# Experts over token lists in DRAM instead of all tokens through all experts

## The chip, the cores and the metric

One core of a Trainium2 chip runs the kernel. The metric is device time in microseconds (us). The engines are TensorE (PE; PEld is its loading of weights), VectorE (DVE), ScalarE (ACT), GpSimd (POOL) and SyncE (SP), which issues most DMAs. Each engine works through its own list of instructions in order; semaphores tie the lists together.

## The reference

2048 tokens of 256 features pass a cross-attention layer with 16 heads over 1601 keys (causal mask and key mask, sigmoid gate, residual), and then a mixture of 8 experts of which each token takes two:

```python
x = x + xattn(layernorm(x), ctx, ctx, mask, Wq, Wk, Wv, Wo, Wg, bg)
xf = layernorm(x)
scores = softmax(xf @ gate_w)                      # (T, 8)
top_scores, top_idx = top_k(scores, 2)
scale = zeros((T, 8)).at[arange(T)[:, None], top_idx].set(top_scores)
xs = scale.T[:, :, None] * xf[None]                # zero rows where not chosen
h = silu(einsum('etd,edh->eth', xs, w1)) * einsum('etd,edh->eth', xs, w3)
x = x + einsum('eth,ehd->etd', h, w2).sum(axis=0)  # hidden size 128
```

An expert gives exactly zero for a token that did not choose it, as silu(0) * 0 = 0.

## The kernel before

The tokens are cut into four chunks of 512 (`CH`), taken in the order 1, 2, 3, 0 (`ORDER`); the chunk 0 is last and has the fewest visible keys. Attention runs over 16 groups (a chunk and four heads): maxima of the scores ("mx", PE and DVE L1303), then per tile of 128 keys the scores ("st", PE L1578), their exponentials (ACT L1160) and the product with the values ("pv", PE L1600). POOL turns a group's maxima into rows for the scores (L1042 to L1055).

After a chunk's attention comes its router: "gT", "wo" (output projection and residual), "bn", "stat" and "norm" (layernorm; POOL's rstd L994), "xT1", "logits", and on DVE the ranks of the 8 probabilities; a rank below 1.5 keeps its probability in `scale_sb` (L1370). "sT" transposes it; it goes to DRAM and comes back as 8 rows broadcast over all partitions ("sload", SP L933).

The feed-forward is dense: for every chunk and every expert, products "a" and "b" (PE L1664 to L1666) of w1 and w3 with all 512 tokens of the chunk, scaled by the token's row on DVE (L1380, L1387), then tanh on ACT, the product of both and "y" with w2 (L1685 to L1693), which sums the 8 experts of a chunk in two banks of PSUM; "yT" transposes back and adds to `x_sb`. Full precision is kept by splitting each operand into a high and a low part (`w_hi`, `w_lo`, `x_hi`, `x_lo`, `h_hi`, `h_lo`), so each product is three matmuls; 32 steps (chunk, expert) of 18 matmuls of 512 columns.

`make_plan` orders all steps ahead of time: a list of streams, each with its needs (`needs`), planned durations (`pe_time`, `ALONE`, `THEN`) and a patience (`PATIENCE`, "feed": 4000 ns). The next step is the one that can start first; among equals, the one whose deadline is nearest. The plan's order is the order of every engine's list; POOL's and SP's lists are sorted by planned start. The experts' weights take the place of keys in SBUF that attention has done with (`freed_by`, "ws" on POOL), and the first of the feed-forward's steps wait until all maxima are done.

Of the kernel before, what the change touches and what calls it, by code (L numbers as in the profile page):

```python
# [34 lines left out]
I32 = mybir.dt.int32  # L35
ALU = mybir.AluOpType
# [31 lines left out]
PATIENCE = {"turn": 1000, "route": 3000, "project": 6000, "weights": 0, "feed": 4000}  # L68
# [3 lines left out]
Y_BANKS = (5, 6)  # L72
# [49 lines left out]
def freed_by(ex):  # L122

    end = 4 * (KD * CH + (ex + 1) * 3 * D if ex is not None else 2 * KD * CH + E * 3 * D)
    return KEYS_LAST + (end - 1) // (4 * (KP - CH)) // 2
# [45 lines left out]
def router(c):  # L171

    return [("gT", c, 0), ("gT", c, 1), ("wo", c, 0), ("wo", c, 1), ("bn", 1, c), ("stat", 1, c),
            ("norm", 1, c), ("xT1", c, 0), ("xT1", c, 1), ("logits", c), ("rexp", c), ("rank0", c), ("rank1", c),
            ("rank", c), ("sT", c)]


def feed_forward():

    steps, todo = [], [(c, e) for c in ORDER for e in range(E)]  # L180
    for i, (c, e) in enumerate(todo):
        if i:
            steps.append(("hl", *todo[i - 1]))
        steps.extend([("a", c, e), ("b", c, e), ("h", c, e)])
        if e == 4 and POS[c] + 1 < NC:
            steps.append(("xs", ORDER[POS[c] + 1]))
        if i >= 3 and todo[i - 3][1] == E - 1:
            steps.extend(finish(todo[i - 3][0]))
        if i >= 2:
            steps.append(("y", *todo[i - 2]))  # L190
            if todo[i - 2][1] == E - 1:
                steps.append(("ycopy", todo[i - 2][0]))
    steps.extend([("y", *todo[-2]), ("hl", *todo[-1]), ("y", *todo[-1]), ("ycopy", ORDER[-1]), *finish(ORDER[-1])])
    return steps


def finish(c):

    return [(kind, c, part) for part in range(2) for kind in ("yT", "out")]


def consumer(e):
# [6 lines left out]
    if kind in ("v", "xT0", "st", "mT", "sT"):  # L209
        return "act"  # L210
    if kind in ("gT", "xT1"):
        return "act" if POS[e[1]] < NC - 1 else "dve"
    return "dve" if kind in ("gate", "mx", "oT", "wo", "logits", "a", "b", "yT") else None


def pe_time(e):
# [7 lines left out]
    if kind == "pv":  # L224
        q0, q1 = shares(e[2], e[3])[e[4]]
        return 4 * PASS * (q1 - q0) + 60
    return {"sel": 230, "v": 860, "gate": 1720, "wo": 1720, "xT0": 450, "xT1": 450, "gT": 450, "oT": 450, "sT": 450, "mT": 230,
            "logits": 900, "a": 1380, "b": 1380, "y": 1400, "yT": 500}.get(kind, 0)


def read_time(e):
# [8 lines left out]
    if kind in ("v", "logits"):  # L240
# [1497 lines left out]
```

## Time and profile before

| | |
|---|---|
| time, three runs | 677.1, 680.0, 682.3 us (median 680.0) |
| span of the profiled execution | 676.9 us; its own time is not listed apart from the three |
| PE | 644.6 us busy (95%), 5320 matmuls |
| PEld | 393.0 us (58%) |
| DVE | 471.3 us (70%) |
| ACT | 379.5 us (56%) |
| POOL | 230.4 us (34%) |
| mean granted PE clock | 0.981 of 2.4 GHz |

The span runs from the first to the last instruction. Busy times of PE are modelled: matmuls overlap, and the sum of single durations is more than the time that they take. The page's slices show DVE full until about 425 us and at 10 to 80% afterwards; PE is full from 40 us to the end.

### The profile page before, as it was taken

The page shows a single profiled execution, that of the slowest core. Times are in us where ns is not written, and L with a number is a line of the kernel's source. Part 1 is how long each engine was busy: PE and PEld are TensorE (multiplying, and loading weights), DVE is VectorE, ACT ScalarE, POOL GpSimd, SP SyncE. Part 2 cuts the span into 40 slices and gives each one's busy share as a digit, 9 for nine tenths or more (in the row PEclk, how much of TensorE's full clock was granted, in tenths as well). Part 3 has the DMA queues.
Part 4 walks back from the last instruction along what each step waited for, and adds up shares of the span by engine and source line. Part 5 has one row for each costly group of instructions (what it writes and reads, how often), then busy time and mean ns, then how long its engine had stood idle before and what let it go on. Part 6 is the DMA issues. An engine that isn't in the chain of part 4 may idle for free.

```text
span 676.9 us, 13559 instructions
## 1 busy us (share of the span) xinstructions
PE 644.6 (95%) x5320; PEld 393.0 (58%) x5320; DVE 471.3 (70%) x981; ACT 379.5 (56%) x778; POOL 230.4 (34%) x283
## 2 busy tenths in 40 slices
PE   7887999999999999999999999999999999979997
PEld 3363565555565545554565556455456766768885
DVE  6637779998989999999989987412205533676454
ACT  2221456766646676667646677877784565123332
POOL 5005212522123115021005033385434434536662
PEclk9878799999999999999999899999999999999999
DMA  6985982010260000010093010102101021104100
GB/s 170 234 133 115 138 144 31 2 22 24 69 68 1 3 1 3 1 65 2 14 161 109 2 34 3 35 2 78 32 32 32 17 63 49 31 16 109 48 32 31
DMA packets 29305, 36.58 MB, mean 54 GB/s; under 512 B 5833, under 2 KB 16457, under 8 KB 29242
## 3 DMA queue, kind: packets, MB, share of 16 engines
q1 hardware_dynamic: 26248, 34.53, 24.6%
q8 instruction: 42, 0.69, 0.4%
q10 hardware_dynamic: 946, 0.92, 0.4%
q0 software_dynamic: 2048, 0.27, 0.3%
q14 instruction: 21, 0.17, 0.1%
HBM read 25.58 MB, written 8.06 MB: 50 GB/s over the span
## 4 chain that ended last, share of the span: by engine, by line
PE 45%; DVE 12%; ACT 3%; POOL 2%; issue 1%; DVEq 0%; ACTq 0%; POOLq 0%
PE bank L1600 9%; DVE pmax L1303 9%; PE bank L1578 8%; PE bank L1664 4%; PE bank L1666 4%; PE bank L1665 4%; PE bank L1429 3%; PE bank L1545 3%; PE bank L1685 2%; PE bank L1686 2%; ACT probs L1160 2%; PE bank L1688 2%; DVE xn_sb L1274 1%; PE bank L1610 1%; PE bank L1583 1%
## 5 line engine op out<-in xcount | busy, mean ns | idle before, releaser
L1160 ACT ACTIVATE probs<-bank 128x512 f32<-128x512 f32 (+4 forms) x592 | 283.2, 555 | 147.0 <-PE bank L1578 87.5
L1303 DVE TENSOR_REDUCE pmax<-bank 128x1 f32<-128x512 f32 (+6 forms) x640 | 322.7, 574 | 29.4 <-PE bank L1549 15.9
L1578 PE MATMUL bank<-qaug,kaug 64*128 64x512 f32 (+4 forms) x592 | 151.6, 455 | 2.5 <-DVE pmax L1303 1.1
L1600 PE MATMUL bank<-probs,vaug 128*32 128x256 f32 (+4 forms) x2048 | 142.3, 390 | 2.2 <-ACT probs L1160 1.8
L1545 PE MATMUL bank<-kaug,qaug 62*128 62x512 f32 (+6 forms) x640 | 135.0, 404 | 9.8 <-DVE stage L807 3.4
L1578 PEld LDWEIGHTS bank<-qaug,kaug 64*128 64x128 f32 (+1 forms) x592 | 66.2, 183 | 85.7 <-ACT probs L1160 29.8
L1545 PEld LDWEIGHTS bank<-kaug,qaug 62*128 62x128 f32 x640 | 76.5, 189 | 40.7 <-DVE pmax L1303 21.0
L1600 PEld LDWEIGHTS bank<-probs,vaug 128*32 128x32 f32 (+1 forms) x2048 | 52.3, 109 | 53.3 <-ACT probs L1160 18.4
L1032 POOL TENSOR_TENSOR h_lo<-v_sb,h_hi 128x512 fp32r<-128x512 f32 x31 | 40.1, 1295 | 66.3 <-ACT h_hi L1216 66.3
L1396 DVE SCALAR_TENSOR_TENSOR v_sb<-t_sb,v_sb 128x512 f32<-128x512 f32 x32 | 24.2, 757 | 45.2 <-POOL v_sb L1028 38.2
L1216 ACT ACTIVATE h_hi<-v_sb 128x512 fp32r<-128x512 f32 x32 | 20.4, 637 | 57.4 <-DVE v_sb L1396 55.5
L1042 POOL TENSOR_SCALAR nmax<-rmax 128x16 f32<-128x16 f32 x16 | 4.4, 278 | 136.3 <-DVE rmax L1311 136.1
L1665 PE MATMUL bank<-x_lo,w_hi 128*128 128x512 f32 x128 | 50.5, 394 | 0.0
L1055 POOL DMA_DIRECT2D qaug<-low_rows x64 | 34.6, 547 | 26.2 <-ACT low_rows L1167 26.2
L994 POOL TENSOR_TENSOR rstd<-var_e,minus_half 128x4 f32<-128x4 f32 x8 | 9.1, 1135 | 83.3 <-DVE var_e L1266 83.3
L1549 PE MATMUL bank<-tri_b,eye_b 64*128 64x128 bf16 (+1 forms) x416 | 37.0, 224 | 0.0
L1387 DVE SCALAR_TENSOR_TENSOR v_sb<-bank,qaug 128x512 f32<-128x512 f32 x32 | 22.1, 689 | 15.2 <-PE bank L1666 15.1
L1093 ACT ACTIVATE stage<-bank 128x512 fp32r<-128x512 f32 (+1 forms) x16 | 8.8, 551 | 37.0 <-PE bank L1429 27.1
L1583 PE MATMUL bank<-eye_b,tri_b 64*128 64x64 bf16 (+1 forms) x416 | 27.9, 195 | 0.0
L1380 DVE TENSOR_TENSOR u_even<-bank,qaug 128x512 f32<-128x512 f32 x16 | 11.0, 688 | 24.0 <-PE bank L1666 24.0
L1380 DVE TENSOR_TENSOR u_odd<-bank,qaug 128x512 f32<-128x512 f32 x16 | 11.0, 687 | 23.9 <-PE bank L1666 23.8
L1685 PE MATMUL bank<-h_hi,w_hi 128*128 128x512 f32 x64 | 26.7, 417 | 0.4 <-ACT h_hi L1216 0.4
(143 smaller groups left out, 824.4 us busy)
## 6 DMA issues: line engine op xcount, KB each, us to landing
qaug<-s_dram SPq DMA_DIRECT2D x32, 256.0 KB, 3.4
qaug<-q_parts SPq DMA_DIRECT2D x18, 256.0 KB, 9.2
q_parts<-stage SPq DMA_DIRECT2D x7, 512.0 KB, 2.9
k_parts<-stage SPq DMA_DIRECT2D x4, 512.0 KB, 5.0
w_sb<-in_w SPq DMA_DIRECT2D x4, 512.0 KB, 10.0
out<-x_sb SPq DMA_DIRECT2D x8, 256.0 KB, 2.3
ctx_sb<-in_ctx_t SPq DMA_DIRECT2D x3, 512.0 KB, 6.4
x_sb<-in_x SPq DMA_DIRECT2D x3, 512.0 KB, 6.3
```

The source lines that it names most:

```text
L1032: pool.tensor_tensor(h_lo[:, i % 2, :], v_sb[:, i % 2, :], h_hi[:, i % 2, :].bitcast(F32), ALU.subtract).then_inc(h_lo_ready, 1)
L1055: pool.dma_start(qaug[row:row + 1, p % 2, GP * g:GP * (g + 1), :].bitcast(F32), m_row[at:at + GP, :].bitcast(F32)).then_inc(m_landed[n % 4 ...
L1160: act.activation(probs[0:rows, u % NSLOT, h, off:CH], bank_of(e)[0:rows, off:CH], ACT.Exp, scale=DK ** -0.5).then_inc(act_read, 1)
L1303: dve.tensor_reduce(pmax[:, n % 2, qt, h, slot:slot + 1], bank[:, 0:w], AX_X, ALU.max).then_inc(dve_read, 1)
L1545: last.append(pe.matmul(pair[side][0][:, 0:w], qaug[b:b + ROW_MAX, p % 2, hp, P * qt:P * (qt + 1)], keys_at(b, ROW_MAX, hp, k0, w), start= ...
L1549: last = [pe.matmul(bank[:, d:w], eye_b[b:b + HALF, a + 1 - side, :], tri_b[b:b + HALF, a + 1 - side, 0:w - d], start=False, stop=(a == 1) ...
L1578: last.append(pe.matmul(pair[side][0][0:r, off:CH], keys_at(b, ROWS, hp, P * j, r), qaug[b:b + ROWS, p % 2, hp, off:CH], start=True, stop= ...
L1583: last = [pe.matmul(bank[0:r, q0:q0 + HALF], tri_b[b:b + HALF, a + 1 - side, 0:r], eye_b[b:b + HALF, a + 1 - side, HALF * a:HALF * (a + 1) ...
L1600: last = pe.matmul(psum[O_BANK][32 * h:32 * h + 32, q0:q1], vaug[0:r, col:col + 32], probs[0:r, u % NSLOT, h, q0:q1], start=(j == 0), stop ...
L1664: pe.matmul(bank[:, :], hi, x_high, start=(a == 0), stop=False)
L1665: pe.matmul(bank[:, :], hi, x_low, start=False, stop=False)
L1685: pe.matmul(dst, hi, h_hi[:, i % 2, :], start=(ex == 0), stop=False)
```

## The change

A token's normalized row is multiplied by each of its two probabilities and written to DRAM, behind the other tokens of that expert. The tokens form three sets: chunks 1 and 2, chunk 3, chunk 0 (`SETS`). For each chunk "cnt" counts on PE, with matrices of ones and of zeros and ones, how many earlier tokens of the set chose each expert; DVE makes a slot number of it for both choices of each token. "wide" makes the weighted rows (on POOL for chunks 1 and 2, on DVE for 3 and 0), and "scat" scatters them with eight indirect DMAs from POOL. "tail" (SP) writes 128 zero rows behind each expert's list, and "table" (DVE) lists for each block of 128 rows which expert it belongs to and where it starts, and for each token where its two results will be.

A set has a fixed number of blocks, two rows per token and up to one started block per expert: 23, 15 and 15, 53 in all. For a block SP reads the row's place into a register and loads 128 rows ("bl"); PE transposes them ("bx") and multiplies them, now as the stationary operand, with 256 columns of w1 and w3 of the block's expert, whose place PE reads from a register ("bab"); "bh" transposes the hidden rows, "by" multiplies with w2; SP stores the result ("bst"). The steps of a block are issued with lags 0 to 3 (`LAGS`). After a set is stored, POOL gathers both results of each token ("back", four indirect DMAs for 256 tokens), and DVE adds them to `x_sb` ("add", "out").

The dense steps ("sT", "sload", "xs", "a", "b", "h", "hl", "y", "ycopy", "yT") are gone. `row_in` and the weights lie in the keys' place. The core of the diff:

```diff
-PATIENCE = {..., "weights": 0, "feed": 4000}
+PATIENCE = {..., "weights": 0, "blocks": 4000}
+SETS = ((1, 2), (3,), (0,))
+LAGS = {"bx": 0, "bab": 1, "bh": 2, "by": 3}
+RING = 3
+COUNT = tuple(2 * TPC * len(chunks) + E - 1 for chunks in SETS)
+BLOCKS = [(s, b) for s, count in enumerate(COUNT) for b in range(count)]
+XIN, YOUT, GOT = 4, 3, 3
+W_STEP = 3 * D
+def block_steps():
+    steps, count = [], len(BLOCKS)
+    for i in range(count + max(LAGS.values())):
+        for kind, lag in LAGS.items():
+            if 0 <= i - lag < count:
+                steps.append((kind, i - lag))
+    return steps
...
-            "logits": 900, "a": 1380, "b": 1380, "y": 1400, "yT": 500}.get(kind, 0)
+            "logits": 900, "cnt": 500, "bx": 280, "bab": 760, "bh": 150, "by": 400}.get(kind, 0)
...
+THEN = {..., "scat": 8800, "back": 4400, "wide": 9800}
...
         if kind == "ws":
-            return [("xs", ORDER[0])] + all_st(freed_by(e[1])) + ...
+            return [("prologue_end",), ("mred", NC * G - 1)] + all_st(freed_by(e[1]))
+        if kind == "bl":
+            s = BLOCKS[e[1]][0]
+            return ([("table", s), ("tail", s)] + [("scat", c) for c in SETS[s]] + all_st(G * (NC - 1) - 1)
+                    + ([("bx", e[1] - XIN)] if e[1] >= XIN else []))
+        if kind == "bx":
+            return [("bl", e[1])] + ([("bab", e[1] - 2)] if e[1] >= 2 else [])
+        if kind == "bab":
+            return [("bx", e[1]), ("ws", E - 1)]
...
# SyncE
+                elif kind == "bl":
+                    i = e[1]
+                    s, b = BLOCKS[i]
+                    if b == 0:
+                        sp.wait_ge(table_ready, s + 1)
+                        sp.wait_ge(tail_out[s], 16 * (E + 1))
+                        for c in SETS[s]:
+                            sp.wait_ge(scattered[c], 16 * 2 * TPC)
+                    if i == 0:
+                        sp.wait_ge(*made(last_st[last_unit[G * (NC - 1) - 1]]))
+                    if i >= XIN:
+                        sp.wait_ge(*taken(("bx", i - XIN)))
+                    at = sp.value_load(read_i[0:1, s, b:b + 1], min_val=0, max_val=E * ROOM[s])
+                    sp.dma_start(row_in[:, i % XIN, :], sent[s][bass.ds(at, 1), :, :].rearrange("r p d -> (r p) d")).then_inc(row_landed[i % XIN], 16)
+                elif kind == "bst":
...
+                    sp.dma_start(fed[s][b, :, :], y_sb[:, i % YOUT, :]).then_inc(y_stored[i % YOUT], 16)
...
# GpSimd
+                elif kind == "scat":
...
+                    for t in range(TPC):
+                        for k in range(2):
+                            pool.wait_ge(rows_wide, 2 * TPC * POS[c] + 2 * t + k + 1)
+                            pool.indirect_dma_start(to, bass.IndirectOffsetOnAxis(ap=slots[:, c, k, t:t + 1], axis=0), wide(k, t), None
+                                                    ).then_inc(scattered[c], 16)
+                elif kind == "back":
...
+                    for r in range(YOUT):
+                        pool.wait_ge(y_stored[r], 16 * sum(1 for i in range(LAST_BLOCK[s] + 1) if i % YOUT == r))
...
+                            pool.indirect_dma_start(got[:, g % GOT, k, t, :], None, rows,
+                                                    bass.IndirectOffsetOnAxis(ap=back_at[:, k, 2 * g + t:2 * g + t + 1], axis=0)
+                                                    ).then_inc(got_landed[g % GOT], 16)
...
# ScalarE: one copy or pass per step of a block
+                    act.activation(row_hi[:, i % 2, :], bank_of(e)[:, 0:D], ACT.Copy).then_inc(row_hi_ready, 1)
...
+                    act.activation(t_sb[:, i % RING, :], bank_of(e)[:, 0:HID], ACT.Tanh, scale=0.5).then_inc(tanh_done, 1)
...
+                    act.activation(h_hi[:, i % RING, :], bank_of(e)[:, 0:P], ACT.Copy).then_inc(h_hi_ready, 1)
...
+                    act.activation(y_sb[:, i % YOUT, :], bank_of(e)[:, 0:D], ACT.Copy).then_inc(act_read, 1)
...
# VectorE, one block
+                    dve.tensor_tensor(row_lo[:, i % 2, :], bank[:, 0:D], row_hi[:, i % 2, :].bitcast(F32), ALU.subtract).then_inc(dve_read, 1)
...
+                    step(dve.scalar_tensor_tensor(out=at_sb[:, i % RING, :], in0=t_sb[:, i % RING, :], scalar=1.0, in1=bank[:, 0:HID],
+                                                  op0=ALU.add, op1=ALU.mult))
+                    dve.scalar_tensor_tensor(out=h_sb[:, i % RING, :], in0=at_sb[:, i % RING, :], scalar=0.5, in1=bank[:, HID:2 * HID],
                                              op0=ALU.mult, op1=ALU.mult).then_inc(dve_read, 1)
...
# TensorE
+                elif kind == "bx":
+                    i = e[1]
+                    pe.wait_ge(row_landed[i % XIN], 16 * (i // XIN + 1))
+                    bank = make(e)
                     for a in range(KD):
+                        last = pe.transpose(bank[:, P * a:P * (a + 1)], row_in[:, i % XIN, P * a:P * (a + 1)], ident[:, :])
                     last.then_inc(dve_full, 1)
+                    s, b = BLOCKS[i]
+                    if b == 0:
+                        pe.wait_ge(table_ready, s + 1)
+                    whose[i] = pe.value_load(whose_i[0:1, s, b:b + 1], min_val=0, max_val=E - 1)
+                elif kind == "bab":
...
                     for a in range(KD):
+                        high, low = (row[:, i % 2, P * a:P * (a + 1)] for row in (row_hi, row_lo))
+                        hi, lo = (w[:, bass.ds(whose[i] * W_STEP + D * a, D)] for w in w_all)
+                        pe.matmul(bank[:, 0:D], high, hi, start=(a == 0), stop=False)
+                        pe.matmul(bank[:, 0:D], low, hi, start=False, stop=False)
+                        last = pe.matmul(bank[:, 0:D], high, lo, start=False, stop=(a == KD - 1))
                     last.then_inc(dve_full, 1)
...
+                elif kind == "by":
...
+                    hi, lo = (w[:, bass.ds(whose[i] * W_STEP + KD * D, D)] for w in w_all)
+                    pe.matmul(bank[:, 0:D], h_hi[:, i % RING, :], hi, start=True, stop=False)
+                    pe.matmul(bank[:, 0:D], h_lo[:, i % RING, :], hi, start=False, stop=False)
+                    pe.matmul(bank[:, 0:D], h_hi[:, i % RING, :], lo, start=False, stop=True).then_inc(act_full, 1)
```

## Rows read from the trace of the kernel before

**Rows 1.** Stretches: us, busy of PE, PEld, DVE, ACT, POOL, clock, DMA, GB/s

```profile
100.00:420.00 320.00, 314.12 (x3128) 177.54 (x3124) 295.14 (x640) 213.98 (x447) 77.72 (x121) 0.99 0.18 33
436.00:607.00 171.00, 163.83 (x1288) 105.86 (x1283) 64.15 (x130) 100.31 (x215) 85.19 (x68) 1.00 0.12 35
607.00:677.00 70.00, 65.01 (x292) 52.18 (x292) 36.49 (x55) 21.14 (x35) 36.96 (x28) 0.99 0.18 53
```

**Rows 2.** One line's instructions: duration ns min/median/max, first and last start

```profile
L1303 DVE TENSOR_REDUCE pmax<-bank x640: 277/546/693, 26.7 to 433.1; 128x1 f32<-128x512 f32 x64, 128x1 f32<-128x364 f32 x48, 128x1 f32<-128x384 f32 x16, 128x1 f32<-128x128 f32 x8
```

**Rows 3.** Stretches, instructions that read or write w_hi (PE, PEld, POOL)

```profile
436.00:607.00 171.00, 69.95 (x208) 38.10 (x208) 21.06 (x16) 1.00 0.12 35
607.00:677.00 70.00, 55.76 (x176) 33.03 (x176) 0.00 (x0) 0.99 0.18 53
```

**Rows 4.** Stretches, instructions that read or write w_lo (PE, PEld, POOL)

```profile
436.00:607.00 171.00, 40.95 (x104) 19.56 (x104) 14.67 (x8) 1.00 0.12 35
607.00:677.00 70.00, 34.81 (x88) 16.53 (x88) 0.00 (x0) 0.99 0.18 53
```

**Rows 5.** Stretches with and without gaps on PE

```profile
20.00:80.00 60.00, 50.98 (x226) 30.95 (x226) 37.83 (x79) 13.88 (x28) 11.46 (x15) 0.83 0.83 160
620.00:640.00 20.00, 20.00 (x88) 16.22 (x87) 10.37 (x13) 5.93 (x10) 14.07 (x11) 1.00 0.15 54
```

**Rows 6.** Two lines' instructions: last step of the choice of experts; a normalization

```profile
L1370 DVE SCALAR_TENSOR_TENSOR scale_sb<-r_rank,r_prob x4: 191/192/193, 227.5 to 607.2; 128x32 f32<-128x32 f32 x4
...
L1274 DVE TENSOR_SCALAR xn_sb<-x_sb,stat,rstd x12: 396/410/1420, 9.1 to 594.0; 128x256 f32<-128x256 f32 x12
```

**Rows 7.** Timeline: start us, us, engine, line, operation, count

```profile
580.36 1.89 PE L1429 MATMUL bank<-wo_sb,att_t 128*128 128x256 f32 x8
...
594.43 0.85 PEld L1504 LDWEIGHTS bank<-ident,xn_sb 128*128 128x128 f32 x8 [2.54 <-DVE xn_sb L1274]
...
597.90 1.98 PEld L1429 LDWEIGHTS bank<-gw_sb,gate_sb 128*128 128x128 f32 x16
```

**Rows 8.** Instruction groups by form: count, busy us, mean ns of one, idle before

```profile
L1160 ACT ACTIVATE probs<-bank 128x128 f32<-128x128 f32 x48 | 10.5, 276 | 10.8 <-PE bank L1583 10.7
...
L1108 ACT ACTIVATE vaug<-bank 128x256 f32<-128x256 f32 x12 | 4.6, 385 | 17.8 <-PE bank L1429 17.8
...
L1323 DVE TENSOR_TENSOR att_sb<-bank,rinv 128x256 f32<-128x256 f32 x16 | 6.8, 425 | 0.6
...
L1303 DVE TENSOR_REDUCE pmax<-bank 128x1 f32<-128x128 f32 x32 | 7.3, 281 | 1.3 <-PE bank L1549 1.3
...
L1004 POOL TENSOR_SCALAR xn_sb<-x_sb,stat,rstd 128x256 f32<-128x256 f32 x20 | 24.3, 1225 | 0.4
...
L1055 POOL DMA_DIRECT2D qaug<-low_rows x64 | 34.6, 547 | 26.2 <-ACT low_rows L1167 26.2
...
L1093 ACT ACT_TABLE_LOAD x1 | 1.3, 1283 | 3.2 <-issue 3.2
```

**Rows 9.** Two lines of DMA issues on SP: duration ns min/median/max

```profile
L933 SPq DMA_DIRECT2D qaug<-s_dram x32: 319/320/441, 388.9 to 634.5; - x32
...
L939 SPq DMA_DIRECT2D out<-x_sb x8: 372/388/389, 555.5 to 674.2; - x8
```

**Rows 10.** The chain of waits around 499 us: start us, us, what

```profile
498.84 0.37 PE bank L1578 x2
...
499.27 0.29 PE bank L1578 x2
...
499.74 1.06 PE bank L1600 x16
```

**Rows 11.** DMA issues: count, KB each, median us to landing

```profile
qaug<-s_dram SPq DMA_DIRECT2D x32, 256.0 KB, 3.4
...
out<-x_sb SPq DMA_DIRECT2D x8, 256.0 KB, 2.3
...
qaug<-low_rows POOLq DMA_DIRECT2D x64, 4.0 KB, 1.6
```

More of the change, by code:

```diff
@@ L35 @@
 I32 = mybir.dt.int32
+U32 = mybir.dt.uint32
 ALU = mybir.AluOpType
@@ L67 @@
 MOST = {"st": 3, "mx": 5}
-PATIENCE = {"turn": 1000, "route": 3000, "project": 6000, "weights": 0, "feed": 4000}
+PATIENCE = {"turn": 1000, "route": 3000, "project": 6000, "weights": 0, "blocks": 4000}
 EPS = 1e-5
@@ L71 @@
 KEYS_LAST = G * (NC - 2)
-Y_BANKS = (5, 6)
+SETS = ((1, 2), (3,), (0,))
+LAGS = {"bx": 0, "bab": 1, "bh": 2, "by": 3}
+RING = 3
+SET_OF = {c: s for s, chunks in enumerate(SETS) for c in chunks}
+ROOM = tuple(TPC * len(chunks) + 1 for chunks in SETS)
+COUNT = tuple(2 * TPC * len(chunks) + E - 1 for chunks in SETS)
+BLOCKS = [(s, b) for s, count in enumerate(COUNT) for b in range(count)]
+LAST_BLOCK = tuple(sum(COUNT[:s + 1]) - 1 for s in range(len(SETS)))
+ROW = D
+XIN, YOUT, GOT = 4, 3, 3
+W_STEP = 3 * D
 Q_PARTS = (0, 0, 1)
@@ L122, in freed_by @@
 def freed_by(ex):
[L124 to L125 removed]
+    return KEYS_LAST + (4 * W_STEP * (ex + 1) - 1) // (4 * (KP - CH)) // 2
 def mate(e):
@@ L267, in make_plan @@
         "project": [[e] for p in range(NC) for e in projections(p)] + [[("prologue_end",)]],
-        "scale": [[("sload", c, ex)] for c in ORDER for ex in range(E)],
         "turn": [[("oT", n)] for n in range(NC * G)],
@@ L275, in make_plan @@
         "values": [[e] for e in values],
-        "weights": [[("xs", ORDER[0])]] + [[("ws", ex)] for ex in range(E)],
-        "feed": [[e] for e in feed_forward()],
+        "weights": [[("ws", ex)] for ex in range(E)],
+        "loads": [[("bl", i)] for i in range(len(BLOCKS))],
+        "blocks": [[e] for e in block_steps()],
+        "stores": [[("bst", i)] for i in range(len(BLOCKS))],
+        "backs": [[("back", *o)] for o in halves()],
+        "adds": [[(kind, *o)] for o in halves() for kind in ("add", "out")],
     }
@@ new lines, in _ @@
+                        dve.wait_ge(*made(("cnt", ORDER[POS[c] - 1])))
+                    dve.tensor_scalar(chosen[:, :, :], r_rank[:, POS[c], :, :], 1.5, None, ALU.is_lt).then_inc(scale_ready, 1)
+                    for k in range(2):
+                        last = dve.scalar_tensor_tensor(out=r_two[:, k, :, :], in0=r_rank[:, POS[c], :, :], scalar=float(k), in1=r_prob[:, :, :],
+                                                        op0=ALU.is_equal, op1=ALU.mult)
+                    step(last)
@@ L1660, in _ @@
+                    pe.matmul(bank[:, 0:TPC, :], above_b[:, :], chosen[:, :, :], start=False, stop=True).then_inc(dve_full, 1)
+                elif kind == "bx":
+                    i = e[1]
+                    pe.wait_ge(row_landed[i % XIN], 16 * (i // XIN + 1))
                     bank = make(e)
                     for a in range(KD):
-                        hi, lo = (w[:, ex, part, HID * a:HID * (a + 1)] for w in (w_hi, w_lo))
-                        x_high, x_low = x_hi[POS[c] % 2][:, a, :], x_lo[:, c, CH * a:CH * (a + 1)]
```

576 lines of the change are left out of this document (311 added, 265 removed).

## Prediction

> **What bounds the kernel now.** I read the stretches first, then the instructions of the feed-forward, then single durations. In the first stretch, 100 to 420 us, TensorE (PE) and VectorE (DVE) are both nearly full: 314 and 295 us of 320 [rows 1]. DVE takes the score maxima, and the last starts at 433 us [rows 2]. From 436 us on DVE has room (64 of 171 us, then 36 of 70), ScalarE too (100 and 21), and PE has none: 164 of 171 and 65 of 70 us [rows 1]. So from 436 us to the end the kernel is a queue of PE work, and a step is worth what it takes or leaves there.
>
> How much of that queue is feed-forward? Its products read w_hi or w_lo: 208 + 104 before 607 us, 176 + 88 after it, 576 in all [rows 3, 4]. The duration a row gives to one is modelled and overlaps the next; the pace is what counts: 20 us that hold 88 matmuls and a full PE give 20 / 88 = 0.227 us, say 0.23 [rows 5]. So the feed-forward takes 312 x 0.23 = 71.8 us of the 171, and 264 x 0.23 = 60.7 us of the last 70, 132.5 us together. The rest of the 171, about 99 us, is the end of attention, the routers of chunks 3 and 0, and small gaps. I cut at 607 because the last choice of experts is written at 607.2 us [rows 6]: from there only experts remain.
>
> **What is removed.** All 576 products, the vector work on 512 columns and the 32 broadcast loads of scale rows. One product of 512 tokens with one expert is 18 matmuls, 4.14 us, or 1.04 us for 128 tokens.
>
> **What is added: 53 blocks on PE.** The count is fixed in the code (23 + 15 + 15), whatever the tokens choose. One block is three transposes and nine matmuls of 256 columns. Eight transposes of that form load in 0.85 us, 0.106 each: 0.32 us [rows 7]. No row has a 256-column matmul of this type. Half of 0.23 is 0.115; the bare weight load, from sixteen 8-column matmuls in 1.98 us, is 0.124; if nothing of the load were hidden, the 256-column matmul of the other float type, eight in 1.89 us, says 0.236 [rows 7]. The load of the 512-column product is hidden (a matmul and its load would not fit into 0.23 one after the other), so I take 0.125: nine are 1.13 us, bounds 1.0 and 2.1. A block is 0.32 + 1.13 = 1.45 us of PE: dearer for 128 rows than the 1.04 of before, but there are 53 and not 128.
>
> **Registers.** Each block loads its expert's number into a register on PE (`value_load`, with every step behind it on PE waiting), forms nine addresses from it, and does the same load for its row on SP. No row shows a register load. Below, it may be hidden, zero: PE's sequencer could run ahead of its products. Above stands the one row of an engine fetching a table before it goes on, 1.28 us [rows 8]. The nearest row is an instruction of a sequencer that talks to something outside its engine, SP's DMA issue of 0.32 us [rows 9]; I take that. Address arithmetic: sixteen loads and sixteen matmuls go in 1.06 us, so a PE instruction needs at most 0.033 us [rows 10]; two steps for nine addresses are up to 0.6 us, of which I count 0.13, the rest hidden behind products. That makes a block T = 1.45 + 0.32 + 0.13 = 1.9 us, from 1.45 to 3.3.
>
> The Trainium skill gives a floor of about 600 ns for a register load ("DMA: Bandwidth & Descriptors", section Latency and other measured facts). No row here shows it; with it T would be 2.05 us and the time 675 us, within 1%.
>
> The other engines stay below T. ACT has two copies of 256 and two passes of 128 columns per block, 2 x 0.385 + 2 x 0.276 = 1.3 us; DVE 0.425 + 3 x 0.281 = 1.3 us [rows 8]; SP two DMA issues, 0.32 + 0.39, and its register load, about 1.0 [rows 9]. The three-block lag of the steps covers the way through them, as long as T stays above about 1.6.
>
> **Added ahead of 436 us.** For chunks 1 and 2 DVE gets some nine small operations each (choice, slots, sums) and one table of about 17: 35 of 0.19 us, the time of such a small one, are 6.7 us, with their waits about 8 [rows 6]. DVE is nearly full there, but scores that PE does meanwhile are not needed later: I count 4 us, bounds 0 and 8. POOL gets the weighted rows (8 x 1.225 = 9.8 us) and the scatters of two chunks [rows 8]; it is busy for 78 of 320 us there [rows 1]. Behind them on POOL wait the steps that turn maxima into score rows; they run ahead of the scores by several groups, which is the cover. Without it each chunk costs up to 15 us.
>
> **When blocks can run.** The first block's load waits for chunk 3's last scores, because its buffers lie in the keys' place. They end at 499 us in before [rows 10], and earlier without the products that ran in between. So attention runs alone from 436 us, and set 0 (23 blocks) and set 1 (15) fill what is left. On POOL a new wait stands: `back` waits until a whole set is stored, and the router's rstd, the gating and the next scatter queue behind it. The order comes from planned times with 1.59 us a block, so a slower T makes this wait late by its excess; PE then still has blocks of the next set.
>
> **The turn at the end.** After the choice for chunk 0 come the count (0.5 us), slots (1.0), a first weighted row (0.41 on DVE [rows 6]), eight scatters, a landing, and a block load. A small POOL DMA holds POOL 0.55 us, a POOL pass over a 128x256 tile 1.225 [rows 8]; eight are 4.4 to 9.8, and I take 8.8, the planner's charge in the diff. Landings are 1.6 to 3.4 us [rows 11]. Sum 0.5 + 1.0 + 0.41 + 8.8 + 2.3 + 0.32 + 2.3 = 15.6 us. Its cover is eight blocks of set 1; I count it as covered.
>
> **The end.** After the last block: copy 0.4, store 0.39 + 2.3, eight gathers 8.8, landing 2.3, two adds of about 0.7, output 0.39 + 2.3: 18.3 us [rows 8, 9, 11].
>
> **The sum.** 436 + 4 + 99 + (53 blocks + 3 rounds to drain) x 1.9 + 18.3 = 440 + 99 + 106.4 + 18.3 = 663.7 us, against this execution's span of 676.9. The median of the runs, 680.0, lies 3.1 above the span, so 667 us. In general the span is 557.3 + 56 T, and it meets the old one at T = 2.14 us. That is a thin margin, since the register price is the least known term.
>
> **Rivals.**
> *Registers on PE's path (slower).* If the load costs half of the 1.28 us, 0.64, and half the arithmetic shows, 0.3, T = 2.39: 691 us of span, 694 us. It ends on the other side from T = 2.14 on. For it: PE is full from 436 us on, and the load stands in the same queue as the products of attention. Against it: PE instructions can queue ahead while products run.
> *The turn is not covered (same).* If set 1 is used up before chunk 0 is chosen, the 15.6 us stand alone: 679 us of span, 682 us. For it: the blocks are taken as soon as PE is free. Against it: attention and router of chunk 0 need PE as well and push blocks back. PE also shows its lower level: from 20 to 80 us, with waits between its products, the granted clock is 0.83 on average, a mix of the levels 1.2 and 2.4 GHz; from 620 to 640, with none, 1.00 [rows 5]. If the last 18 rounds ran at 1.2 GHz, they would cost up to 1.0 us more each, and this case ends slower. The Trainium skill says the same of the default state: an idle TensorE is gated to half rate ("TensorE: Matmul & The Clock Gate", Part 1: The HAM clock gate). By that rule this rival would take 18 us more; the 0.83 agrees.
> *All of it hidden (faster by more).* With T = 1.45 the span is 638 us, 642 us.
>
> **Chances.** Forecast (T from 1.6 to 2.1, turn covered) 0.42; registers 0.28; turn bare 0.18; all hidden 0.12. Faster by over 1% (below 673 us) needs T below 2.01: 0.36 of the forecast and the 0.12, so 0.48. Within 1% (about what a measurement of this kernel tells from no change): 0.06 of the forecast, 0.02 of the registers, 0.13 of the turn, 0.21. Slower: 0.26 + 0.05 = 0.31. The forecast's own range is 650 to 678. The range with the others goes from 640 (T = 1.43) to 706 (T = 2.6); the dearest register prices and the clock at 1.2 GHz through the last set lie outside.
>
> **What would show it.** In the profile after: twelve matmuls per block and what stands on PE's sequencer between blocks (the register load's own row); the start of the first block, about 485 us; maxima ending near 437 us; the pace of the set-0 blocks; PE's idle time between the choice for chunk 0 and its first block, and the granted clock there; POOL's time for one scatter; the 18 us after the last block. I am wrong if a block takes over 2.14 us of PE's time, if POOL's longer queue holds up the scores before 436 us, or if PE stands idle around the last scatter.

## The result and the profile after

The change made no difference of use: 682.2 us (median of 12 runs, 680.4 to 685.5) against 680.4 us before (12 runs), a ratio of 1.0045 [1.0027, 1.0064]. The forecast was 667 us. The profiled execution has a span of 680.1 us; the sum had 663.7, so 16.4 us have to be found. One execution of a variant further down (table_later: 967 us, against 675 to 681 us in its nine others) is left out of its ratio.

The same stretches as in [rows 1], cut where the kernel after has its turning points (its last maximum, the first block of set 1, the last result copied from PSUM). Columns: stretch, us, busy of PE, PEld, DVE, ACT, POOL, granted clock, DMA share, GB/s.

```profile
100.00:420.00 320.00, 309.76 (x2997) 172.64 (x2989) 294.55 (x651) 207.53 (x434) 103.23 (x140) 0.98 0.19 41
446.00:576.00 130.00, 117.50 (x1227) 75.89 (x1225) 55.81 (x204) 96.48 (x255) 40.91 (x40) 1.00 0.20 65
576.00:661.00 85.00, 62.94 (x380) 54.73 (x380) 50.27 (x174) 36.80 (x127) 31.44 (x32) 0.84 0.57 174
661.00:680.00 19.00, 0.00 (x0) 0.00 (x0) 2.77 (x4) 0.09 (x1) 7.89 (x8) 0.50 0.32 97
```

Up to 576 us the kernel after is ahead: chunk 0's last choice of experts is written at 575.0 us, not 607.2 [rows 6]. Then the blocks of sets 1 and 2 run alone, PE is busy for 63 of 85 us at a granted clock of 0.84 (a mix of 1.2 and 2.4 GHz), and the lead is gone. Before, PE was nearly full to the end, 65 of 70 us at 0.99 [rows 1].

The maxima end at 446.1 us instead of 433.1 [rows 2]. One line's instructions: durations in ns, first and last start.

```profile
L1392 DVE TENSOR_REDUCE pmax<-bank x640: 278/547/693, 26.6 to 446.1; 128x1 f32<-128x512 f32 x64, 128x1 f32<-128x364 f32 x48, 128x1 f32<-128x384 f32 x16, 128x1 f32<-128x128 f32 x8
```

What PE waited for between 576 and 661 us (engine, line, releaser: us in all, times, longest):

```profile
PE bank L1835 <- DVE row_lo L1548: 6.6, 4, 3.3
PE bank L1849 <- DVE h_lo L1563: 5.9, 5, 3.0
PE bank L1835 <- DVE h_sb L1556: 2.4, 5, 0.6
PE bank L1843 <- DVE h_sb L1556: 2.0, 2, 1.7
PE bank L1835 <- ACT y_sb L1302: 1.9, 7, 0.3
PE bank L1819 <- DMA row_in<-sent: 1.7, 1, 1.7
PE bank L1835 <- DVE h_lo L1563: 1.0, 2, 0.7
```

Some 22 us, 17.9 of them for DVE, which itself is busy for only 50 of the 85 us. So DVE is not too slow; something else stands ahead of the blocks' steps in its list. Two things do. First, the adds. The chain of waits (start us, us, what):

```profile
636.24 5.11 DMA gate_sb<-fed,back_at
...
641.38 0.70 DVE x_sb L1569
...
642.71 0.29 DVE h_lo L1563
```

The gather takes 5.1 us from its issue to its landing. The add (L1569) that needs it stands in DVE's list ahead of a block's `h_lo`, so DVE sits idle for the last 2.4 us, and PE's next product waits for that `h_lo`. Four such waits take 8.0 us between 576 and 661 us (timeline of DVE, then its waits):

```profile
641.38 0.69 DVE L1569 TENSOR_TENSOR x_sb<-gate_sb,x_sb 128x512 f32<-128x512 f32 x1 [2.42 <-DMA gate_sb<-fed,back_at]
```

```profile
DVE x_sb L1569 <- DMA gate_sb<-fed,back_at: 8.0, 4, 3.2
```

Second, chunk 0's table, 19 small steps in one piece. The timelines of DVE and PE (start us, us, engine, line, operation; in brackets idle time and releaser):

```profile
582.36 0.18 DVE L1507 TENSOR_TENSOR filled<-in_blocks,number 128x32 f32<-128x32 f32 x1
...
586.14 0.22 DVE L1541 TENSOR_REDUCE back_at<-behind 128x8 uint32<-128x64 f32 x1
586.27 0.41 DVE L1548 TENSOR_TENSOR row_lo<-bank,row_hi 128x256 fp32r<-128x256 f32 x1
...
586.83 0.58 PE L1835 MATMUL bank<-w_hi,row_hi 128*128 x1 [3.31 <-DVE row_lo L1548]
```

SyncE has a third such piece: the eight tails of chunk 0, each behind a register load, during which it loads no rows and stores no results (timeline of SP, 8.4 us for `x8`):

```profile
579.40 0.43 SPq L1010 DMA_DIRECT2D fed<-y_sb  x1
579.94 0.37 SPq L986 DMA_DIRECT2D sent<-none_sb  x1
581.22 8.40 SPq L989 DMA_DIRECT2D sent<-none_sb  x8
589.66 0.45 SPq L1010 DMA_DIRECT2D fed<-y_sb  x1
591.45 0.36 SPq L1004 DMA_DIRECT2D row_in<-sent  x1
```

Behind the longer of these pauses the granted clock drops. Two 20 us windows (columns as above):

```profile
580.00:600.00 20.00, 13.83 (x71) 12.67 (x70) 11.57 (x49) 6.95 (x24) 12.09 (x13) 0.66 0.65 211
600.00:620.00 20.00, 12.81 (x79) 11.02 (x78) 12.02 (x33) 7.78 (x27) 11.78 (x12) 0.83 0.75 218
```

A block at the lower level takes 2.56 us (transposes at 596.69 and 599.25), at the higher one 1.87.

### The profile page after: what moved, and what is told of

Its sections match the earlier page's. It is cut to its first block and busy times, and to the rows that moved or that the text cites. A ratio compares the mean times of both kernels' runs of the same rounds, so it can differ in the third digit from the quotient of the medians.

```text
span 680.1 us, 15375 instructions
## 1 busy us (share of the span) xinstructions
PE 601.9 (89%) x5356; PEld 367.8 (54%) x5356; DVE 489.1 (72%) x1214; ACT 391.9 (58%) x910; POOL 220.2 (32%) x306
## 5 line engine op out<-in xcount | busy, mean ns | idle before, releaser
L1702 PE MATMUL bank<-kaug,qaug 62*128 62x512 f32 (+6 forms) x640 | 137.7, 408 | 13.5 <-DVE pmax L1392 5.6
L1835 PE MATMUL bank<-w_hi,row_hi 128*128 x106 | 37.5, 354 | 14.6 <-DVE row_lo L1548 6.6
L1137 POOL DMA_INDIRECT gate_sb<-fed,back_at x32 | 31.4, 981 | 52.4 <-issue 34.4
L1162 POOL DMA_DIRECT2D qaug<-m_row x64 | 34.7, 548 | 33.5 <-ACT m_row L1274 33.5
L1290 ACT ACTIVATE t_sb<-bank 128x128 f32<-128x128 f32 x53 | 15.0, 283 | 42.2 <-PE bank L1837 42.1
L1176 POOL TENSOR_TENSOR att_sb<-att_sb,gate_sb 128x256 f32<-128x256 f32 x16 | 11.7, 732 | 72.5 <-DVE att_sb L1412 72.0
L1835 PEld LDWEIGHTS bank<-w_hi,row_hi 128*128 128x128 f32 x106 | 22.3, 211 | 22.5 <-issue 22.1
L1548 DVE TENSOR_TENSOR row_lo<-bank,row_hi 128x256 fp32r<-128x256 f32 x53 | 22.2, 420 | 15.5 <-PE bank L1819 7.6
L1836 PE MATMUL bank<-w_hi,row_lo 128*128 x106 | 31.9, 301 | 0.0
L1837 PE MATMUL bank<-w_lo,row_hi 128*128 x106 | 31.9, 301 | 0.0
L1554 DVE SCALAR_TENSOR_TENSOR at_sb<-t_sb,bank 128x128 f32<-128x128 f32 x53 | 15.1, 285 | 23.0 <-ACT t_sb L1290 21.6
```

The lines of the kernel that those rows point to most:

```text
L1137: pool.indirect_dma_start(got[:, g % GOT, k, t, :], None, rows, bass.IndirectOffsetOnAxis(ap=back_at[:, k, 2 * g + t:2 * g + t + 1], axis= ...
L1162: pool.dma_start(qaug[row:row + 1, p % 2, GP * g:GP * (g + 1), :].bitcast(F32), m_row[at:at + GP, :].bitcast(F32)).then_inc(m_landed[n % 4 ...
L1548: dve.tensor_tensor(row_lo[:, i % 2, :], bank[:, 0:D], row_hi[:, i % 2, :].bitcast(F32), ALU.subtract).then_inc(dve_read, 1)
L1702: last.append(pe.matmul(pair[side][0][:, 0:w], qaug[b:b + ROW_MAX, p % 2, hp, P * qt:P * (qt + 1)], keys_at(b, ROW_MAX, hp, k0, w), start= ...
L1835: pe.matmul(bank[:, 0:D], high, hi, start=(a == 0), stop=False)
L1836: pe.matmul(bank[:, 0:D], low, hi, start=False, stop=False)
```

## The experiments

Letters name the theories. A: DVE's list (adds, chunk 0's table) holds up the blocks of sets 1 and 2. B: POOL's longer list holds up the maxima. C: register loads on PE set the pace. D: DMA traffic is the limit. E: the tails on SyncE. F: the first set's table on DVE holds up the maxima. The ratio is to the kernel before, with its 95% interval. The last three columns are from each kernel's profiled execution: the start of the last maximum, of the first block of set 1, and from there to the start of the last copy out of PSUM (30 blocks and the drain). Longer lags let the first block of set 1 start up to three rounds earlier and add three rounds of drain, so the last two columns are compared among kernels of the same lags: lags_two and all from moved_all on have the longer ones, but for zero_short.

| kernel | ratio | maxima end | set 1 starts | to the last result |
|---|---|---|---|---|
| after | 1.0045 [1.0027, 1.0064] | 446.1 | 576.4 | 84.3 |
| adds_later | 0.991 [0.988, 0.994] | 448.4 | 578.5 | 73.7 |
| lags_two | 0.993 [0.989, 0.998] | 446.2 | 571.6 | 82.6 |
| scat_later | 0.995 [0.991, 0.998] | 438.1 | 571.6 | 82.4 |
| no_register | 0.997 [0.994, 1.001] | 446.7 | 576.5 | 83.0 |
| table_later | 0.995 [0.991, 0.998] | 436.8 | 570.5 | 83.9 |
| scat_only | 0.997 [0.994, 1.001] | 441.9 | 573.1 | 82.9 |
| zero_alone | 1.001 [0.998, 1.004] | 450.3 | 581.6 | 80.6 |
| moved_all | 0.975 [0.972, 0.978] | 436.1 | 565.3 | 75.1 |
| moved_out | 0.971 [0.967, 0.975] | 433.9 | 562.9 | 73.7 |
| moved_table | 0.973 [0.970, 0.976] | 437.1 | 566.1 | 77.2 |
| moved_four | 0.991 [0.988, 0.993] | 436.7 | 574.4 | 80.9 |
| moved_zero | 0.971 [0.966, 0.975] | 440.2 | 568.0 | 69.5 |
| zero_short | 0.981 [0.977, 0.985] | 445.4 | 577.9 | 71.0 |
| zero_table | 0.967 [0.961, 0.974] | 443.2 | 570.7 | 66.7 |
| table_scat_early | 0.978 [0.973, 0.983] | 452.7 | 578.1 | 67.6 |
| table_no_register | 0.960 [0.954, 0.966] | 440.9 | 567.4 | 62.3 |
| zero_late | 0.961 [0.957, 0.965] | 435.4 | 563.1 | 67.5 |

**One thing alone.** The adds, planned later:

```diff
-            at = on_pool(e, at) + (HOP if kind in ("scat", "back") else 60)
+            at = on_pool(e, at) + (HOP if kind == "scat" else 12000 if kind == "back" else 60)
```

> The plan charges 12 us instead of 2.5 us for the landing of a gather, so VectorE's adds stand some four blocks later in its list. Theory A (VectorE's list: in 576 to 661 us TensorE waits 22 us, 17.9 of them for VectorE, because adds that wait for a gather stand ahead of block work): the waits behind adds, 7 us in 600 to 620 and 5 us in 638 to 650, go, and some of the 1.2 GHz stretches behind them: 664 to 672 us. Theory C (register loads on TensorE set the pace of a block) and theory D (the DMA traffic of gathers, scatters and loads is the limit): no change, 680 to 684 us.

673.6 us, 1.6 us above theory A's range and well below the 680 to 684 us of C and D. The stretch from set 1 on is 10.6 us shorter, and among its blocks DVE no longer waits for any gather (8.0 us in the kernel after). D falls with it, since the same bytes are moved. The output DMAs move with the adds, and SyncE's wait for adds between 560 and 660 us falls too, from 9.7 to 6.0 us; moved_out below bears on that.

Longer lags between a block's steps:

```diff
-LAGS = {"bx": 0, "bab": 1, "bh": 2, "by": 3}
+LAGS = {"bx": 0, "bab": 2, "bh": 4, "by": 6}
```

(`row_hi` and `row_lo` get three buffers.)

> The steps of a block are issued with lags 0, 2, 4, 6 instead of 0, 1, 2, 3, and the split rows get three buffers instead of two, so each block has about 2.7 us more for ACT and VectorE between two of its steps. Theory A: TensorE no longer feels a pause of VectorE of up to some 2.7 us (table, weighted rows, most adds): 12 to 20 us less, 662 to 670 us. Theory C: the pace of an undisturbed block stays 1.87 us and three more rounds of drain are added: 682 to 688 us. Theory D: no change, 680 to 684 us.

674.8 us: 7.4 us better than the kernel after, but less than the 12 to 20 that A had said. The last result is copied at 654.2 us instead of 660.7. DVE still waits 8.3 us for gathers, up to 2.5 at a time, and the two adds behind such a wait take 1.4: together more than the cover of 2.7. PE also waits 3.2 us for one row load.

No register on PE:

```diff
-                    whose[i] = pe.value_load(whose_i[0:1, s, b:b + 1], min_val=0, max_val=E - 1)
+                    whose[i] = i % E
```

> TensorE takes expert i mod 8 for block i, fixed ahead of time, and loads no register; which expert's weights a block meets is the part of the computation that is changed. Theory C (the register load and the addresses cost 0.3 to 0.5 us of TensorE's path in each of 53 blocks): the undisturbed pace falls from 1.87 to about 1.4 us and the time by 10 to 20 us, 662 to 672 us. Theory A: the pace falls in the undisturbed stretch (some 8 blocks), but where VectorE holds the blocks up nothing is won: 674 to 680 us.

The pace is as C says, the time as A says. Timelines of PE where nothing disturbs the blocks, first the kernel after, then no_register: a block's transposes, its first product (or the next block's), and the next transposes.

```profile
630.47 0.38 PE L1819 MATMUL bank<-ident,row_in 128*128 128x128 f32 x2
631.13 0.38 PE L1835 MATMUL bank<-w_hi,row_hi 128*128 x1 [0.28 <-ACT y_sb L1302]
...
632.41 0.38 PE L1819 MATMUL bank<-ident,row_in 128*128 128x128 f32 x2
```

```profile
630.46 0.38 PE L1819 MATMUL bank<-ident,row_in 128*128 128x128 f32 x2
630.60 0.36 PE L1835 MATMUL bank<-w_hi,row_hi 128*128 128x256 f32 x1
...
631.85 0.38 PE L1819 MATMUL bank<-ident,row_in 128*128 128x128 f32 x2
```

In the kernel after 0.66 us lie between the transposes and the first product, without the register 0.14; a mean undisturbed block takes 1.87 and 1.42 us. The load has a row of its own, and a register operation stands behind each (kernel after, ns min/median/max):

```profile
L1824 PEldq TENSOR_LOAD <-whose_i x53: 296/303/722, 496.2 to 654.6; - x53
L1824 PEldq FUSED_REGOPS  x53: 151/151/165, 496.8 to 655.1; - x53
```

53 blocks by 0.45 would be 24 us, yet the whole gains 4.4 us on the kernel after (677.8 against 682.2), and the stretch from set 1 on 1.3: from 576 us on PE waits 21 us for DVE and 5 for row loads, instead of 18 and 2. Where the queues set the pace, a cheaper block is worth little.

**Why the maxima are late.** I first took POOL's list to be the cause:

```diff
+   ... + ([("mred", NC * G - 1)] if kind == "wide" and e[1] == ORDER[1] else [])
```

> The weighted rows and the scatters of chunk 2 wait on POOL until the last maxima are reduced. Theory B (the maxima end at 446 us instead of 433 us because on POOL the 14.7 us of weighted rows and 10.2 us of scatters stand ahead of the step that turns group 11's maxima, for which VectorE and the scores wait): the last maximum ends at 433 to 438 us and TensorE is full from 400 to 420 us; the first block comes up to 10 us later, so the whole is 674 to 684 us. Without B (the small VectorE operations of the routers made the maxima late): the last maximum stays at 444 to 447 us.

The maxima ended at 438.1, as B said. But the first set's table stands behind the scatters in the list of steps, and it had moved with them, from 405 to 444 us. So two more kernels move one of the two each:

```diff
+            ... + ([("mred", NC * G - 1)] if kind == "table" and not e[1] else [])
```

> The kernel after, with one step moved: the table of the first set, on VectorE, waits until the last maxima are reduced; weighted rows and scatters of chunk 2 stay where they are on POOL. In scat_later this table had moved too, since it stands behind the scatters in the list of steps. Theory F (the table, 7.6 us in one stretch on VectorE from 400.7 to 408.3 us, holds up the maxima): they end at 436 to 440 us. Theory B (POOL's list): 444 to 447 us.

> The kernel after, with weighted rows and scatters of chunk 2 behind the last maxima on POOL, and the table of the first set ahead of them at its old place on VectorE. Theory B (POOL's list holds up the step that turns the maxima): the maxima end at 436 to 440 us. Theory F (the table on VectorE): 444 to 447 us, and the whole about that of the kernel after or, as the first rows come later, up to 5 us more.

With the table alone moved they end at 436.8 us: theory F, and B's rows and scatters are covered. One line's instructions in table_later, to be held against the 446.1 us of the kernel after:

```profile
L1392 DVE TENSOR_REDUCE pmax<-bank x640: 276/545/693, 26.6 to 436.8; 128x1 f32<-128x512 f32 x64, 128x1 f32<-128x364 f32 x48, 128x1 f32<-128x384 f32 x16, 128x1 f32<-128x128 f32 x8
```

scat_only met neither number, 441.9 us, and shows why. DVE and POOL in the kernel after, then DVE in scat_only, where POOL does nothing meanwhile (timelines):

```profile
400.67 0.21 DVE L1507 TENSOR_TENSOR filled<-in_blocks,number 128x64 f32<-128x64 f32 x1
...
403.17 1.72 DVE L1523 TENSOR_TENSOR inside<-number,begun 128x23 f32<-128x23 f32 x1
404.92 0.18 DVE L1524 SCALAR_TENSOR_TENSOR place_f<-which,inside 128x23 f32<-128x23 f32 x1
405.14 1.50 DVE L1526 TENSOR_SCALAR read_i<-place_f 128x23 int32<-128x23 f32 x1
405.23 1.42 DVE L1530 TENSOR_SCALAR room_of<-number 128x8 f32<-128x8 f32 x1
...
406.72 0.71 DVE L1534 SCALAR_TENSOR_TENSOR shift<-start_of,room_of 128x8 f32<-128x8 f32 x1
...
408.12 0.29 DVE L1541 TENSOR_REDUCE back_at<-behind 128x16 uint32<-128x128 f32 x1
...
403.79 2.81 POOL L1174 TENSOR_SCALAR gate_sb<-gate_sb 128x1024 f32<-128x1024 f32 x1
406.68 0.72 POOL L1176 TENSOR_TENSOR att_sb<-att_sb,gate_sb 128x256 f32<-128x256 f32 x1
```

```profile
391.35 0.21 DVE L1507 TENSOR_TENSOR filled<-in_blocks,number 128x64 f32<-128x64 f32 x1
...
393.85 0.18 DVE L1523 TENSOR_TENSOR inside<-number,begun 128x23 f32<-128x23 f32 x1
...
394.28 0.18 DVE L1526 TENSOR_SCALAR read_i<-place_f 128x23 int32<-128x23 f32 x1
...
395.49 0.28 DVE L1541 TENSOR_REDUCE back_at<-behind 128x16 uint32<-128x128 f32 x1
```

The table takes 4.4 us by itself (in scat_only, where it also starts 9 us earlier) and 7.7 us beside POOL's gating, because steps of 0.18 us then last 1.4 to 1.7. Against table_later the maxima are 5.1 us late with the short table and 9.3 with the long one. In the kernel after PE stops for 3.3 us at the table's end, and its clock between 400 and 420 us is 0.83.

**What the causes are worth together.** moved_all joins adds_later, lags_two and scat_later; moved_out also plans the output's DMA 8 us later in SyncE's list:

```diff
-            on_sp(e, at)
+            on_sp(e, at + (8000 if kind == "out" else 0))
```

> The later adds, the lags 0, 2, 4, 6 and the later scatter of chunk 2 together. Each alone took 4 to 6 us off. If they mend separate places the sum is 15 us, 663 to 667 us; if the later adds and the longer lags mend the same pauses of VectorE (theory A in both), the larger of the two and the scatter remain: 668 to 671 us.

> As moved_all, and the output's DMA is planned 8 us later in SyncE's list. In lags_two SyncE waited 11.6 us for an add with the next row loads queued behind it, and TensorE waited 3.2 us for a row load. If SyncE's list is what is left: 2 to 5 us below moved_all. If the four row buffers cover it: within 1 us of moved_all.

663.5 us, in the range for separate places. By the ratios, each against the kernel after, the three single savings add up to 0.034, and together they give 0.030; the larger of A's two and the scatter alone would give 0.023. So the causes lie for the most part in separate places. moved_out's 660.2 is in the range of its theory, but the intervals of the two overlap, so SyncE's wait for the adds is not shown to matter.

moved_table spreads chunk 0's table over the blocks, three steps behind each; moved_four loads four experts at one place:

> As moved_all, and chunk 0's table is no longer one stretch of 4 us on VectorE: three of its steps follow each block's work. Theory A (that stretch stops TensorE for 3.3 us in the kernel after, and the clock falls to its lower level behind it): 3 to 7 us below moved_all, and the granted clock in 580 to 600 us near 1.00. If the longer lags already cover it: within 1 us.

> As moved_all, and TensorE loads the experts of four blocks into registers at one place instead of one at each block. A load costs 0.45 us of TensorE's path (1.87 against 1.42 us per block). If loads one behind the other overlap, the mean pace falls to some 1.55 us and the time by 2 to 8 us against moved_all. If each pays in full, the mean pace stays at 1.87 us, one block in four takes about 3.2 us, and the time is that of moved_all or up to 4 us more.

moved_table gains nothing by itself (663.3 us), but not because the lags cover the table: in its profile PE waits 9.6 us for one row load. With DVE's pause gone, SyncE's tails (theory E), which take 9.5 us there, stop the blocks. moved_four is 11.5 us slower than moved_all, more than either case. The pause at one place of loads (timeline of PE, moved_four):

```profile
615.76 0.38 PE L1837 MATMUL bank<-w_hi,row_hi 128*128 x1 [2.05 <-issue]
```

The block with the loads takes 3.7 us (transposes at 613.3 and 617.0), the others 1.40: 2.3 us for four loads, 0.57 each. They don't overlap, and the pause is longer than what queued products cover.

Theory E: the areas of sets 1 and 2 are zeroed ahead by one DMA each (at about 395 us), and their tails leave SyncE's list:

```diff
+                    for later in range(1, len(SETS)):
+                        rows = E * ROOM[later] + 1
+                        sp.dma_start(sent[later].rearrange("r p d -> p r d"), none_sb[:, :].unsqueeze(1).to_broadcast([P, rows, ROW])
+                                     ).then_inc(tail_out[later], 16)
```

> The kernel after, but the row areas of the second and third set are zeroed by one DMA each behind the first set's tail at about 395 us; their own tails on SyncE are gone. Theory E (chunk 0's eight tails hold SyncE from 581.2 to 589.6 us, so that no row is loaded and no result is stored): the gap in the blocks between 583 and 596 us shrinks by 3 to 8 us, 675 to 679 us. Theory A alone (the table on VectorE stops the blocks over the same time anyway): 680 to 682 us.

> As moved_out, with the early zeroing. Theory E: the wait of 3.2 us for a row load and most of the 1.2 GHz stretch behind it go, 4 to 8 us below moved_out, 652 to 656 us. If the table on VectorE stops the blocks just as long: within 2 us of 660 us.

> As moved_zero, with chunk 0's table in steps of three behind each block's work. With both causes gone (A's 4 us on VectorE, E's 8.4 us on SyncE) the blocks of the second set run at 1.9 us each and the granted clock stays near 1.00 from 560 to 620 us: 2 to 5 us below moved_zero. If the longer lags cover the table: the same as moved_zero within 1 us.

> As moved_zero, but with the lags 0, 1, 2, 3 and two buffers of the change as it was. If the longer lags are what covers VectorE's pauses: 4 to 8 us above moved_zero. If adds and tails were the whole of it: the same or 1 to 3 us less, as the drain is shorter.

zero_alone: 1.001, by its time theory A alone. The columns say more: the stretch from set 1 on is 3.7 us shorter, as E said, but set 1 starts 5.2 us later. moved_zero against moved_out is the same: 4.2 us shorter, 5.1 later, no gain in sum. With table and tails both out of the way (zero_table) the stretch falls to 66.7 us, clock 1.00 in both windows from 580 to 620 us. From the first block of set 1 to the last block (29 steps) it takes 58.6 us, 2.02 for each; the kernel after takes 78.5 us, 2.71 for each. The time of zero_table, 658.0 us, is 2.4 below moved_zero, with intervals that overlap. zero_short, with the old lags, takes 7.4 us more than moved_zero: the longer lags do cover the short pauses, once the long ones are gone. A part of the 7.4 may be its maxima, 5.2 us later in the profile; but from the first block of all to the last result it is still 6.2 us longer (499.0 to 648.9 us against 493.8 to 637.5).

Two runs on top of zero_table, one without the register, one with chunk 2's scatters and the first set's table back at their old places:

> As zero_table, but TensorE takes expert i mod 8 for block i and loads no register (which expert's weights a block meets is changed). Alone this saved 2 us, though a block fell from 1.87 to 1.42 us. If the queues' stalls had taken that gain, it comes back once they are gone: the 29 steps from the first block of the second set to the last block fall from 53.6 us to 41 to 46 us, 645 to 651 us in all. If something else (row loads, VectorE or ACT at 1.3 us per block) sets the pace: over 50 us and 655 to 658 us.

> As zero_table, but chunk 2's weighted rows and scatters stand where the change put them on POOL, ahead of group 11's maxima. Theory B with an effect on the end: the maxima end 8 to 12 us later than in zero_table and the whole takes 3 to 7 us more, 661 to 665 us. If the time between the maxima and the first block is set by ACT's exponentials anyway: within 2 us of zero_table.

Without the register the time falls to 652.8 us, by 5.3: neither case, and hardly more than the 4.4 us that it gave alone. (In zero_table the 29 steps take 58.6 us, not the 53.6 of the expectation; here they take 54.7.) So the lost gain does not come back with the stalls gone: the 30 blocks gain 4.4 us of the 13.5 that 0.45 us each would give. What keeps the rest is open; now PE waits for row loads (4.5 us). table_scat_early costs 8.5 us, 1.5 more than its range: the late maxima (452.7 against 443.2 us) are paid at the end.

Is the zeroing itself what makes set 1 start late? zero_late lets it wait for the last maxima:

```diff
+                    sp.wait_ge(mx_reduced, NC * G)
                     for later in range(1, len(SETS)):
```

> As zero_table, but the early zeroing (10.8 MB) starts only when the last maxima are reduced. In zero_table it moved 200 to 330 GB/s from 400 to 440 us; there TensorE waited 3.7 us for a score row and the maxima ended at 443 us, against 434 to 438 us without the zeroing. If the zeroing's traffic caused that: maxima at 434 to 438 us and 3 to 6 us below zero_table, 652 to 655 us. If the spread of executions did: within 1.5 us of 658 us.

Yes: the maxima end at 435.4 us, and the time is 653.6 us, ratio 0.961 [0.957, 0.965], the best version that computes the whole reference. 400 to 440 us in zero_table, then in zero_late (stretch, us, busy of the engines, clock, DMA share, GB/s):

```profile
400.00:440.00 40.00, 35.35 (x436) 20.14 (x428) 25.62 (x68) 25.08 (x48) 14.82 (x30) 0.91 0.85 282
```

```profile
400.00:440.00 40.00, 38.82 (x480) 21.81 (x480) 30.44 (x80) 30.38 (x59) 16.29 (x36) 1.00 0.08 23
```

And the stretch of sets 1 and 2 in zero_late, to be held against 576 to 661 us of the kernel after:

```profile
563.00:631.00 68.00, 55.54 (x403) 47.27 (x401) 52.31 (x187) 37.43 (x135) 31.88 (x32) 1.00 0.66 203
```

85 us at a clock of 0.84 have become 68 at 1.00, with the same blocks, the same registers and nearly the same bytes (203 GB/s over 68 us are 13.8 MB, 174 over 85 us are 14.8).

## Why the prediction was wrong

The sum, term by term, against the profiled execution of the kernel after:

| | forecast | measured |
|---|---|---|
| start of set 1: 440 + 99 + 23 x 1.9 | 582.7 | 576.4 |
| 30 blocks and 3 rounds: 33 x 1.9 | 62.7 | 84.3 |
| the end | 18.3 | 19.4 |
| span | 663.7 | 680.1 |

**Up to set 1.** "I count 4 us, bounds 0 and 8" for the work ahead of 436 us was 13 us [rows 2]; table_later shows that 9 of them are the first set's table, which I had counted among 35 small operations of 0.19 us and not as one piece of 7.7. What the text feared, POOL's longer queue, is covered, as it said, but for its part in that piece: beside POOL's work the table is longer by 3 us. The 99 us of other work came out near 86 (130 us from 446 to 576, less 23 blocks of 1.9), though PE was not full there as I had it: from 446 to 500 us ACT sets the pace with its exponentials.

```profile
446.00:500.00 54.00, 46.97 (x562) 20.87 (x564) 3.41 (x11) 51.77 (x110) 25.07 (x25) 1.00 0.04 12
```

ACT is busy for 51.8 of 54 us, PE for 47. The dense steps of before had filled such gaps; the blocks can't, as they need the keys' place. The kernel before, 440 to 500 us, PE busy for 59.3 of 60:

```profile
440.00:500.00 60.00, 59.26 (x512) 31.16 (x516) 11.21 (x18) 47.70 (x97) 33.09 (x30) 1.00 0.11 32
```

So the first block came at 497.5 and not at 485. Part of the attention had run beside the longer maxima, as the text assumed, and the net is 6.3 us in its favour.

**A block.** T was right: 1.9 us forecast, 1.87 measured undisturbed; products and transposes 1.45 forecast, 1.42 without the register; register and addresses 0.32 + 0.13 forecast, 0.45 measured. That the second sum fits so well is partly luck. The 0.32 was the row of a DMA issue, and the load's own row happens to be as long, 0.30. The addresses cost nothing that shows: blocks of moved_four that load nothing form them too, and take 1.40 us. What shows beside the load is the register operation of 0.15 behind it, which the sum did not have. The rival with registers on PE's path (T = 2.39) is out: the load is on the path, but at the price taken. The Trainium skill states a floor of about 600 ns for a `tensor_load` ("DMA: Bandwidth & Descriptors", section Latency and other measured facts). The trace does not agree: its TENSOR_LOAD takes 0.30 us, and only a load together with what stands behind it comes near, 0.57 us of each in moved_four. The 2.05 us that the prediction drew from that floor leave out its own 0.13 for addresses; with them the estimate by that page would have been 2.18 us and a time of 682 us, and the measured block of 1.87 us rules it out.

**The step that failed** is "+ 56 T" itself, with "the three-block lag of the steps covers the way through them" and "I count it as covered". The engines' busy times per block (ACT and DVE 1.3 us) are below T, but I had looked for waits only on POOL, where `back` stands. Each list takes its own in order: DVE's adds wait for gathers (moving them makes this stretch 10.6 us shorter, adds_later), chunk 0's table is a piece of 4 us there, and on SP I counted two issues and a load per block and left out the tails, eight loads and DMAs in 8.4 us. These pauses overlap, so they don't add up one by one. With all of them out of the way and longer lags (zero_table) the 29 steps take 58.6 us instead of 78.5, so the pauses and the clock behind them are some 20 of the 21.6 us. How much of it is the clock was not measured apart. A mean of 0.84 over 85 us is 27 us at the lower level; ten blocks there, at 2.56 instead of 1.87 us, would be 7 us, an estimate from these numbers.

**The turn.** The rival "the turn is not covered" gave 682 us and the time is 682.2, but not by its mechanism, so that the number fits is chance: set 1's last block began at 620.5 us, and the last row was scattered at 590. From the choice to the end of the last scatter it took 15.4 us (575.0 to 590.4), where the sum had 10.7; it was covered all the same, but its parts lie on the lists that the covering blocks use. The third sign of being wrong came true, for PE stands idle for 3.3 us up to 586.8 us, while the scatters run; what it waits for is the table and not the rows. The rival's clock at 1.2 GHz is what happened, mostly in set 1 (0.66 and 0.83 in the two windows above) and little in the last (0.91 from 620 to 660 us).

**The end.** 19.4 us against 18.3: scatters came every 1.27 us and gathers every 1.25, so the last eight gathers took 10.0 us, not 8.8.

```profile
L1137 POOL DMA_INDIRECT gate_sb<-fed,back_at x32: 942/947/1372, 594.6 to 673.3; - x32
L1569 DVE TENSOR_TENSOR x_sb<-gate_sb,x_sb x8: 683/692/693, 601.9 to 676.1; 128x512 f32<-128x512 f32 x8
```

## What to carry to other kernels

Work that is "covered" still stands in an engine's list: for every step that waits for a DMA, and every run of small steps, ask which instructions of the covering work stand behind it, on DVE and on the queue that issues loads too. When a pipeline loses time in many places, single repairs show little, since the next wait takes their place: compare stretches of the traces, not only times, and repair together. The price of one block can be forecast to 2%, here with some luck, and the time still miss, if the pace is set by order and not by work.

## What was not expected of the hardware

- Small DVE steps that read and write SBUF stretch beside a POOL tensor operation: 0.18 us became 1.4 to 1.7 beside a POOL pass of 2.8 us. The Trainium skill names a cause ("Trainium Architecture — The Big Picture", section What this means for kernel authors): DVE and GpSimd share a port pair, and the holder locks it out for the other. The trace agrees in part: most of the long steps end with a POOL pass (406.6 and 407.4 us), but one ends at 404.9 in the middle of a pass, and the step behind it takes its usual 0.18. I had not drawn on it.
- Register loads on PE don't overlap: four in a row cost 2.3 us, one at a time 0.45 each, though the load itself takes 0.30.
- An indirect DMA of 128 rows of 1 KB holds POOL for 0.95 us and comes every 1.25 to 1.27 us, in scatters and gathers alike.
- PE's granted clock fell behind pauses of 2 to 3 us among the blocks (0.66 in 580 to 600 us), and without them stayed at 1.00 with PE busy for 55.5 of 68 us.
